# A four-network GNN kernel: the column loop of its PNA layers as straight code, with one wide maximum

## The reference, cut to what matters

```python
msg = concatenate([h[src], h[dst]], axis=-1) @ Mw.T + Mb
deg = segment_sum(ones(E), dst)
s1, s2 = segment_sum(msg, dst), segment_sum(msg * msg, dst)
mx, mn = segment_max(msg, dst), segment_min(msg, dst)
mean = s1 / deg
var = relu(s2 / deg - mean * mean)
std = sqrt(var + 1e-30)
agg = concatenate([mx, mn, std, var], axis=-1)
h_neigh = concatenate([agg, agg * (log(deg + 1) / 4), agg * (4 / log(deg + 1))], axis=-1)
u = concatenate([h, h_neigh], axis=-1) @ Uw.T + Ub
```

## Time and profile before

| | |
|---|---|
| median of 3 runs | 3951.08 us (3942.02 to 3959.58) |
| the profiled execution's own time | 3915.32 us |
| its span | 3913.5 us |
| PE busy | 2472.3 us (63%) |
| DVE busy | 2233.6 us (57%) |
| ACT busy | 692.3 us (18%) |
| POOL busy | 1258.7 us (32%) |
| mean granted TensorE clock | 0.785 |

### The profile page before, as it was taken

One profiled execution on the slowest core, in us unless ns is written; L12 is line 12 of the kernel. 1 busy time (PEld: TensorE's weight loads), 2 busy tenths in 40 slices (PEclk: granted clock), 3 DMA queues, 4 the chain that ended last, 5 costly groups with the idle time before them and its releaser, 6 DMA issues. The chain is left out here.

```text
span 3913.5 us, 50857 instructions
## 1 busy us (share of the span) xinstructions
PE 2472.3 (63%) x11996; PEld 1384.5 (35%) x11997; DVE 2233.6 (57%) x6995; ACT 692.3 (18%) x1557; POOL 1258.7 (32%) x1321
## 2 busy tenths in 40 slices
PE   6988879886968955455456654454448644544563
PEld 2444345743635532222224422222225322222242
DVE  6877766463353265555555645555556645555555
ACT  0235532411121030000001500000003300000112
POOL 3000000002000036666642155655640356555520
PEclk8999989997979977677678676766767867767785
DMA  3122366253523535444441144444430444444411
GB/s 109 50 93 109 142 210 230 99 206 124 176 81 138 176 100 179 159 163 159 138 145 40 53 160 144 160 155 135 157 113 1 141 136 160 154 134 158 153 43 45
DMA packets 152225, 511.54 MB, mean 131 GB/s; under 512 B 32194, under 2 KB 51552, under 8 KB 151248
## 3 DMA queue, kind: packets, MB, share of 16 engines
q1 hardware_dynamic: 94782, 350.03, 25.5%
q0 software_dynamic: 43536, 93.43, 8.6%
q10 hardware_dynamic: 13826, 67.12, 4.2%
HBM read 280.33 MB, written 230.13 MB: 130 GB/s over the span
## 5 line engine op out<-in xcount | busy, mean ns | idle before, releaser
L615 POOL DMA_INDIRECT rows_g<-a_dram,idx_now x1173 | 1133.3, 966 | 1566.8 <-DMA a_dram<-g 801.4
L1485 PE MATMUL psum<-hs,slab 128*128 128x384 bf16 x6600 | 1196.2, 341 | 166.2 <-issue 124.0
L1485 PEld LDWEIGHTS psum<-hs,slab 128*128 128x128 bf16 x6600 | 674.5, 102 | 711.2 <-issue 326.3
L1045 DVE SCALAR_TENSOR_TENSOR run<-run,mask_pt,rows_g 128x128 f32<-128x128 f32 x1170 | 405.6, 347 | 278.5 <-issue 224.7
L1048 DVE SCALAR_TENSOR_TENSOR run<-run,mask_pt,rows_g 128x128 f32<-128x128 f32 x1170 | 403.3, 345 | 34.6 <-issue 26.8
L1637 PE MATMUL psum<-identity,std_now 128*128 128x128 f32 x75 | 33.6, 448 | 598.1 <-ACT std_now L1341 512.9
L1432 PE MATMUL psum<-onehot_key,onehot_lane 128*128 128x512 bf16 (+1 forms) x1968 | 366.4, 343 | 60.9 <-issue 36.3
L726 DVE TENSOR_SCALAR onehot_key<-key_row,key_at 128x1600 bf16<-128x1600 f16 x492 | 310.2, 630 | 0.0
L1644 PE MATMUL psum<-w_U,vturned 128*128 128x384 f32 x150 | 119.2, 896 | 292.6 <-ACT vturned L1349 265.2
L1341 ACT ACTIVATE std_now<-var_now,eps 128x128 f32<-128x128 f32 x75 | 30.1, 401 | 1444.5 <-DVE var_now L1007 928.9
L1432 PEld LDWEIGHTS psum<-onehot_key,onehot_lane 128*128 128x128 bf16 x1968 | 160.4, 100 | 249.5 <-issue 55.0
(11 more groups left out here) (298 smaller groups left out, 3018.2 us busy)
## 6 DMA issues: line engine op xcount, KB each, us to landing
slab<-at_part SPq DMA_DIRECT2D x200, 800.0 KB
scan_dram<-run SPq DMA_DIRECT2D x291, 512.0 KB
at_part<-part_now ACTq DMA_DIRECT2D x50, 800.0 KB, 3.6
sums_dram<-run ACTq DMA_DIRECT2D x43, 576.0 KB, 2.9
rows_g<-a_dram,idx_now POOLq DMA_INDIRECT x1173
rows_g<-in_attr SPq DMA_DIRECT2D x43, 148.5 KB
a_dram<-g SPq DMA_DIRECT2D x3, 1600.0 KB, 7.7
agg<-sel_dram SPq DMA_DIRECT2D x3, 1600.0 KB
```

The costliest lines, as they stand in the source:

```text
L615: nc.gpsimd.indirect_dma_start(rows_g[:, slot, j, :], None, a_dram, bass.IndirectOffsetOnAxis(ap=idx_now[:, slot, j:j + 1], axis=0)).then_ ...
L1045: V.scalar_tensor_tensor(at[:, 0:D], before[:, 0:D], mark, rows, ALU.add, ALU.max).then_inc(s_run, 1)
L1485: T_.matmul(ps[:, 0:3 * D], counts[:, k * P:(k + 1) * P], hs[:, k, at:at + 3, :].rearrange("p s f -> p (s f)"), start=(k == 0), stop=False ...
```

## The change

The loops of POOL, DVE and ACT over the columns are written out, with constants in place of registers. A gather takes its index straight from `src_pt`; it may start once DVE has done the group four before. It writes the first half of a row in `rows_g`, which is now twice as wide; ACT writes the negated values into the second half (one operation for a group), and DVE makes one maximum of 256 values a column over both: the minimum is kept as the maximum of the negated values and turned back in the merges. The writes of `run` go out from ACT's queue, one group later, and SP only loads slabs.

Of a block, the own node's row is added to the sums by two identity products on PE; DVE has one reduction (`sums_of`), ACT the square of the mean, DVE one subtraction (`variance`), ACT Relu and root. Each step has a fixed group: the sums after group min(4b+3, 3b+24), variance and square one later, Relu and root two later, and both ACT's `var_turned(b)` and DVE's `take_part(b)` three later (two for the last two blocks). `take_part` has three operations; the biases' rows are added by a product with one row of ones into `bu`, for which PE's wait for the layer's weights moves ahead. Small tiles move into the unused third slab.

```diff
+def sums_at(b):
+    return min(4 * b + 3, 3 * b + 24)
+def take_at(b):
+    return sums_at(b) + (3 if b < NB - 2 else 2)
...
-        idx_now = sb("idx_now", [P, RING, Q], I32)
-        rows_g = sb("rows_g", [P, RING, Q, D], F32)
+        rows_g = sb("rows_g", [P, RING, Q, 2 * D], F32)
...
 @block.sync
-                with sp.Fori(0, TURNS) as turn:
-                    for k in range(2 * RING):
-                        write_runs(2 * RING * turn + RING, k)
-                        if k % RING == 0:
-                            half = k // RING
-                            load(2 * turn + (3 + half), 1 - half, turn + (1 + half))
+                with sp.Fori(1, NB // 2) as turn:
+                    for half in range(2):
+                        load(2 * turn + half, half, turn)
+                load(NB - 1, 0, NB // 2)
+                sp.wait_ge(s_run, T * l + T)
...
 @block.gpsimd
-                    pool.wait_ge(s_idx, GT * l + first + (k + 1))
+                for k in range(GT):
+                    slot = k % RING
+                    if k >= RING:
+                        pool.wait_ge(s_run, T * l + Q * (k - RING) + Q)
+                    elif l:
+                        pool.wait_ge(s_run, T * l)
+                        pool.wait_ge(s_st[slot], written_before(l, slot))
+                    for j, t in enumerate(cols_of(k)):
                         nc.gpsimd.indirect_dma_start(
-                            rows_g[:, slot, j, :], None, a_dram,
-                            bass.IndirectOffsetOnAxis(ap=idx_now[:, slot, j:j + 1], axis=0)).then_inc(s_gat[slot], 16)
+                            rows_g[:, slot, j, 0:D], None, a_dram,
+                            bass.IndirectOffsetOnAxis(ap=src_pt[:, t:t + 1], axis=0)).then_inc(s_gat[slot], 16)
...
 @block.vector
+                def sums_of(b):
+                    ps = psum[:, 1024 + 1024 * (b % 2):2048 + 1024 * (b % 2)].rearrange("p (k c) -> p k c", k=2)
                     dve.wait_ge(s_spmm, n + (NB * 5 + 4))
+                    V.tensor_reduce(var_tmp[:, 2 * (b % 2):2 * (b % 2) + 2, :],
+                                    ps[:, :, 0:3 * D].rearrange("p k (s f) -> p k f s", s=3), AX.X,
+                                    ALU.add).then_inc(s_agg, 1)
+                def variance(b):
+                    dve.wait_ge(s_mean_sq, n + 1)
+                    V.scalar_tensor_tensor(var_raw[:], var_tmp[:, 2 * (b % 2) + 1, :], rdeg[:, b:b + 1], mean_sq[:],
+                                           ALU.mult, ALU.subtract).then_inc(s_var, 1)
                 def take_part(b):
                     dve.wait_ge(s_vmm, n + 2)
-                    V.tensor_tensor(row(edge_sum, b), row(edge_sum, b), lrows[:, 0, :], ALU.add)
...
-                    V.tensor_tensor(u0, u0, lrows[:, 1, :], ALU.add).then_inc(s_vu, 1)
+                def columns(k):
+                    dve.wait_ge(s_minus_rows, GT * l + k + 1)
+                    if l or k >= RING:
+                        dve.wait_ge(s_st[slot], 16 * (k // RING) + written_before(l, slot))
+                    for j, t in enumerate(cols_of(k)):
+                        dve.wait_ge(s_run, T * l + t)
+                        V.scalar_tensor_tensor(at, before, mask_pt[:, t:t + 1], rows, ALU.add,
                                                ALU.max).then_inc(s_run, 1)
+                for k in range(GT):
+                    columns(k)
+                    for b in range(NB):
+                        if sums_at(b) == k:
+                            sums_of(b)
+                        if sums_at(b) + 1 == k:
+                            variance(b)
+                        if take_at(b) == k:
+                            take_part(b)
...
 @block.scalar
-                with act.Fori(0, NB) as b:
-                    deviations(b)
-                    var_turned(b)
+                for k in range(GT):
+                    slot, n = k % RING, len(cols_of(k))
+                    act.wait_ge(s_gat[slot], gathered_before(l, slot) + 16 * Q * (k // RING) + 16 * n)
+                    A.mul(rows_g[:, slot, 0:n, D:2 * D], rows_g[:, slot, 0:n, 0:D], -1.0).then_inc(s_minus_rows, 1)
+                    if k:
+                        write_runs(k - 1)
+                    for b in range(NB):
+                        if sums_at(b) + 1 == k:
+                            mean_squared(b)
+                        if sums_at(b) + 2 == k:
+                            deviations(b)
+                        if take_at(b) == k:
+                            var_turned(b)
+                write_runs(GT - 1)
...
 @block.tensor
+                if c >= CALLS:
+                    for ps, at in zip(banks, ats):
+                        T_.matmul(ps[:, 0:3 * D], identity16[:],
+                                  hs[:, ds(b, 1), at:at + 3, :].rearrange("p b s f -> p (b s f)"), start=False,
+                                  stop=False, skip_group_check=True)
...
                     T_.matmul(bank(6 + b % 2)[:, 0:2 * D], ft2[:, b * P:(b + 1) * P], weights["M"][:, D:3 * D],
-                             start=True, stop=True).then_inc(s_bu, 1)
+                             start=True, stop=False)
+                    T_.matmul(bank(6 + b % 2)[:, 0:2 * D], ones[0:1, :], both, start=False, stop=True).then_inc(s_bu, 1)
```

More of the change, by code:

```diff
@@ L272, in gnn_kernel @@
         esum = run[:].rearrange("p r q f -> p (r q f)")[:, 0:3 * EC * D].rearrange("p (s j f) -> p s j f", s=3, j=EC)
-        same = var_tmp[:].rearrange("p k f -> p (k f)")[:, 0:T]
-        same_turn = std_now
-        ecarry_t = vturned[:, 0:P + 1]
-        ecarry = var_now
+        beside = rows_flat[:, 4 * ET * P:]
+        same = beside[:, 0:T]
+        same_turn = beside[:, 512:512 + P]
+        ecarry_t = beside[:, 768:768 + P + 1]
+        ecarry = beside[:, 1024:1024 + P]
         s_last = sem("s_last")
@@ L964, in told @@
                     return V_LAYER * l + V_X3 + k
-                def take_indices(first, k):
-                    n = len(cols_of(k)) if isinstance(first, int) and first == 0 else Q
-                    V.tensor_copy(idx_now[:, k % RING, 0:n], src_pt[:, ds(Q * first + Q * k, n)]).then_inc(s_idx, 1)
-                if l:
-                    dve.wait_ge(s_run, 2 * T * l)
-                for k in range(RING):
-                    take_indices(0, k)
                 for b in range(NB):
@@ L1023, in take_part @@
-                    dve.wait_ge(s_take, 3 * n + 6)
-                    V.tensor_tensor(u0, u0, lrows[:, 1, :], ALU.add).then_inc(s_vu, 1)
-                def columns(turn, k):
-                    slot = k % RING
-                    whole = turn is None
-                    i = k if whole else 2 * RING * turn + (RING + k)
-                    n = len(cols_of(k)) if whole else Q
-                    rounds = k // RING if whole else 2 * turn + (1 + k // RING)
-                    full = 16 * Q * rounds
-                    dve.wait_ge(s_gat[slot], full + (gathered_before(l, slot) + 16 * n))
-                    dve.wait_ge(s_st[slot], 16 * rounds + written_before(l, slot))
-                    for j in range(n):
+                    dve.wait_ge(s_take, 2 * n + 2)
@@ L1046, in columns @@
                                                ALU.max).then_inc(s_run, 1)
-                        dve.wait_ge(s_run, steps)
-                        V.scalar_tensor_tensor(at[:, D:2 * D], before[:, D:2 * D], mark, rows,
-                                               ALU.subtract, ALU.min).then_inc(s_run, 1)
-                    if not whole or k + RING < GT:
-                        dve.wait_ge(s_run, 2 * Q * i + (2 * T * l + 2 * n))
-                        if whole:
-                            take_indices(0, k + RING)
-                        else:
-                            take_indices(2 * RING * turn + RING, k + RING)
@@ L1057, in _ @@
-                for k in range(RING):
-                    columns(None, k)
-                variances(0, 0)
-                with dve.Fori(0, TURNS) as turn:
-                    for half in range(2):
-                        for k in range(RING * half, RING * half + RING):
-                            columns(turn, k)
-                        take_part(2 * turn + half)
-                        variances(2 * turn + (half + 1), 1 - half)
-                for k in range(FIRST, GT):
-                    columns(None, k)
-                    if k in (FIRST + 1, FIRST + 4):
-                        b = 2 * TURNS + (k - FIRST) // 3
-                        take_part(b)
-                        variances(b + 1, (b + 1) % 2)
+                for k in range(GT):
[7 more added lines that the diff above has]
+                            take_part(b)
@@ L1072, in _ @@
                 take_part(NB - 1)
                 dve.wait_ge(s_last_turned, l + 1)
[L1075 to L1077 removed]
+                for e in range(2):
+                    last = V.tensor_tensor_scan(carry_t[:, e, 1:P + 1], mask_turn[:], bank(0)[:, e * P:(e + 1) * P],
```

(12 more changed lines are left out.)

131 lines of the change are left out of this document (46 added, 85 removed).

## The result

The changed kernel takes 4015.75 us (4009.18 to 4026.22, 4 runs) where the kernel before takes 3953.57 us (3942.02 to 3959.58, 4 runs): a ratio of 1.0163, 95% interval 1.0131 to 1.0196, so it is slower by 62 us. Its profiled execution took 4009.18 us for a span of 4007.2 us. The profiled execution of before was 38 us under its median and this one 7 us under, so the two profiles differ by more, 93.7 us, than the medians. Most of the experiments ran on chips where both kernels are far faster, because nothing is held up there beside the gathers; each of them stands beside the kernel before on its own chip.

The account below looks back on a forecast made before the run. Bound by a chain: POOL's gathers plus pauses for late index copies. Gathers 1485, pauses 442 and ends' wait 63 make 1990 against 1951.8 us, +38, so 3951 + 38 = 3989 us; range 3800 to 4235.

Parts of the forecast that it names:

- The hold-up: Gather streaks some 7 us old: PE's counts unseen until 2.8 us (up to 4.3) after the streak ends; DVE's sequencer crawls.
- The gathers' pace (3523): Rival, column loops: pauses were only the loops' own, so straight code runs at 1485 + 39 us; -428, chance 0.14.
- the rule of the Trainium skill, "Runtime: NRT & Kernel Launch", section "Instruction fetch mechanics": Taken branches out of a two-page window stall fetch; by that, straight code would remove all DVE's issue, giving 3523.
- The pause for each block, 6.4 us in 69: Column loops: POOL stops after 16 gathers for DVE's late take_part, 6.4 us a block, 442 us in all.
- their count is written at 8.4 us, beyond the age: PE's products in a block, counted 8.4 us (7.5 to 8.7) after POOL's restart, too late to be seen at once.
- seen in time in some blocks: Rival, column loops: some blocks' PE products are seen within the streak; -28, 3923 us, chance 0.20.
- The pause after a late transpose: Rival, column loops: transposes' count also late, ACT stands in var_turned; 9.8 us a block, +262, 4213 us, chance 0.14.
- The bias product: 256-column PE product, 25 a layer beside the first streak: under 1.0 us each, 0 in the sum.
- The ends' wait: POOL's wait for the last run writes before the ends' gathers: raised from 53.0 to 63 us.
- The wide maximum: One 256-wide DVE maximum a column: 467 ns, 0.50 us with release against 0.53 for two; saves nearly nothing.
- The 1485 us of the gathers: POOL in the three loops: 1173 gathers at 1.27 us from start to start, unchanged by the change.
- pauses and start: Column loops: 69 pauses of 6.4 us (442) replace 414 us of pauses; the start stays the same.

Follow-up runs that it names:

- y2: The kernel before, unchanged, profiled again on a chip where nothing is held up: 3383.73 us, one run.
- x1: Changed kernel without the product that adds the bias rows (part of the answer left out), nothing held up: 3386.35 us, ratio 1.0006 to before.
- w3: The kernel before with only the bias rows' product added in place of DVE's two operations, counts held up: 3924.03 us, ratio 1.0057 to before.
- y1: The changed kernel, unchanged, on a chip where nothing is held up: 3456.62 us, ratio 1.0206 to before.
- y3: Changed kernel with bias rows added by two DVE operations again, without the one-row product, nothing held up: 3393.13 us, ratio 1.0026 to before.
- w1: z1 with the 256-wide maximum split into two of 128, on a chip where counts are held up: 3936.85 us, ratio 1.0087 to before.
- z1: Changed kernel with bias rows on DVE and run writes on SP's queue again, nothing held up: 3392.28 us, ratio 1.0030 to before.
- y4: Changed kernel with the run writes on SP's queue again, nothing held up: 3446.04 us, ratio 1.0187 to before.
- x4: Changed kernel with the blocks' DVE and ACT calls and PE's transposes and products with U out of the loop: 3447.46 us, one run.
- x3: Changed kernel with POOL filling 256 unused values after each group of four gathers, nothing held up: 3532.52 us, ratio 1.0426 to before.

## Why the prediction was nearly right, and where it was not

Forecast were 3989 us and 0.47 for slower; measured were 4015.75 and 62 us instead of 38. The time fell inside the range, but in good part by luck: the pattern of the pauses was another one, and what was missed lies in terms put at 0 and +10.

**The hold-up: there, but only half described, and its cause open.** In an older streak the others go on waiting for PE until some microseconds past its end. The prediction put this to counts that are not seen and left PE's matmuls at their usual pace. In the result that fits 18 of 36 waits; in the other 18 the transposes themselves end late, because PE itself crawls ahead of them, at up to 2.9 us a matmul. The kernel before had this in the stretch of the earlier trace rows too: 11 matmuls of the block products in the 2 us from 890.61, then one every 0.7 to 2.8 us until 915.09.

y2 tests what the hold-up costs, and whether it is the code's: the same instructions with the same gathers, and 531 us less, 1951.8 - 1531.7 = 420 of them in the loops. Of the other 111, 28 are lost ahead of the edge gathers, where DVE's busy time is about half of y2's only from 25 to 75 us, at the program's first 25 gathers and just behind them; 23 come between the start of the edge gathers and the first loop, and 61 behind the three loops, where 25 gathers each stand. So it is not the code alone, and the time is lost beside gathers and just behind them. The lower clock of the held-up kind is not what costs the time: PE's busy time in a loop is 322 to 324 us there and 314 to 315 in y2.

That the gathers cause it rests on these times; no run changed them where the hold-up is. A rival stays untested: that the sequencers of PE, DVE and ACT are all slowed together, instead of PE's counts being kept back. What makes an execution one or the other is open too; it went with the chip (3383 and 3384 on two, 3901 and 3954 on others), and x1's one long execution, without a profile, is the only one that left its chip's level. Everything in the prediction was argued for the kind that the result was measured on.

**The gathers' pace (3523), given 0.14.** Straight code alone did not bring it, and the rule of the Trainium skill, "Runtime: NRT & Kernel Launch", section "Instruction fetch mechanics", explains nothing where nothing is held up: the looped kernel runs at the gathers' pace in y2. Where PE crawls it does not fit either: in the result's profile the two instruction queues moved 103 packets in all, and PE has 296 issue gaps ahead of one line. Where nothing is held up both kernels are at that pace, and the change still loses 2%.

**The pause for each block, 6.4 us in 69: the pattern failed, the sum held.** The step "their count is written at 8.4 us, beyond the age" was sized too late: it is seen at 7.6 us, so every other block passes, and the second has its transposes late. This is the rival "seen in time in some blocks", in every second block. Two blocks take 40.9 + 11.7 = 52.6 us, against 2 x 26.7 = 53.4 by the forecast: less than 1 us a block between them, but not for the priced reason, so that the sum held is luck. The pause after a late transpose was put at 9.8 us and is 11.2 to 13.2: ACT goes on 4.3 to 6.5 us after a streak of 32, not 2.8; the other steps (0.4, 2.9, 1.0, 2.0) are as worked out. In POOL's idle time: 33 pauses of 11.8 are 390 us, where 442 were forecast; 67 us of waits after the first 16 gathers come to them.

**The bias product: mis-sized, the largest miss.** "Under 1.0 us, beside the first streak, 0 in the sum." At the full clock it adds little: the first blocks follow each other at 1.26 us instead of 0.8 on the mean. But with it PE has no gap left, the granted clock falls from 1.00 to 0.50, and the rest follow at 2.30 us: 32.7, 25.6 and 25.7 us more for the 25 blocks, where the prediction had at most 25. And the cover was never the 41 us of the first streak: in both kernels POOL needs DVE's first columns after 16 gathers, and the streak of before is 32 long only because DVE comes in time. With DVE late, POOL stands 27.5, 19.8 and 19.8 us. An estimate from these rows: 24 steps of 1.26 us would be 30.2 us instead of 52.5, 45.4 and 45.5, and the waits some 5 us each, so most of the late start is the clock. In place of DVE's two operations it costs 22.6 us where counts are held up (w3) and 63.5 us where not (y1 to y3).

**The ends' wait: +10 forecast, +34.6 measured.** The timelines of PE, DVE and POOL at the end of the last loop, whose last gather ends at 3789.26:

```profile
3797.44 8.66 PE L1469 MATMUL psum<-hs,slab 128*128 128x384 bf16 x48
...
3797.68 0.35 DVE L995 SCALAR_TENSOR_TENSOR ft<-psum,log,ft 128x128 f32<-128x128 f32 x1 [22.47 <-PE psum L1636]
...
3809.08 0.35 DVE L995 SCALAR_TENSOR_TENSOR ft<-psum,log,ft 128x128 f32<-128x128 f32 x1 [5.29 <-PE psum L1636]
...
3812.88 1.52 DVE L1016 SCALAR_TENSOR_TENSOR run<-run,mask_pt,rows_g 128x256 f32<-128x256 f32 x3
...
3818.91 0.95 POOL L625 DMA_INDIRECT hs<-scan_dram,end_idx  x1 [29.66 <-DMA scan_dram<-run]
```

From the last gather to DVE's take_part at 3797.68 it is 8.4 us (PE ends the transposes at 3794.20, 4.9 us after the last gather; then the copy and the products). Then DVE's take_part at 3809.08 waits 5.29 us for the next block's products, and PE has a whole block of matmuls (8.66 us) ahead of them; the last columns stand behind that operation, end at 3814.40, and their write lands 4.5 us later. I had counted one late block after the last gather, and there are two, one after the other. In w1, on another chip, with the same order on DVE and the writes on SP's queue, the three waits are 15.7, 30.2 and 15.3 us, 61.2 in all; what share the queue has in that stays open.

**The wide maximum: 467 ns forecast, 485 measured;** no gain from it, as said. The gathers grew by 17 ns, 20 us in all, where I had left them as they were. Where nothing is held up there are more long gathers with the wide operation (over 1.06 us, 251 of 1248 in y3, 90 in y2); in y3 they lie beside DVE operations for 0.68 of their time and the short ones for 0.50. DVE's company alone can lengthen a gather: the program's first 25 take mostly 1.11 us in y2, with DVE 22.3 of 25 us busy, and mostly 0.95 in the kernel before, with DVE at 10.1. The Trainium skill, "SBUF — State Buffer", section "SBUF: two separate sides", lets a two-input DVE operation and a GpSimd one that reads SBUF exclude each other, which would lengthen a gather that meets a longer operation. The runs don't settle it: with the wide operation the mean is 983 ns in the result, 984 in x1, y1 and z1 and 986 in y3, but 972 in y4, 979 in x4 and 969 in x3; with narrow ones 963 in w1, 966 and 969 in the kernel before and w3, 975 in y2. The cause of the 20 us stays open.

**The sum.** The 1485 us of the gathers are 1173 x 1.266; with the rounded 1.27 that is written there they would be 1490, on both sides of the difference. By terms, in the two profiles: gathers +20 (forecast 0), pauses and start +37 (+28), ends +35 (+10), 92 against 38. Against the medians the miss is 62 to 38, since the profiled execution of before was a quick one. The experiments give a rough split on another chip of that kind (before 3901): w1, which leaves out the bias product, the queue and the wide operation, +35; the bias product, put into the kernel before, +23. That they nearly add up to 62 proves nothing, since they start from different kernels.

No version was faster than the kernel before: y3 and z1 are 0.3% slower where nothing is held up, and w1 0.9% where it is. None of them ran on the other kind.

## What to carry to other kernels

Ask of a stretch that covers a step what makes it as long as it is: here the cover itself hung on the engine that the step made late. Ask of a small product added to PE whether PE still has gaps, and read the granted clock of that stretch afterwards: here the clock, and not the product's columns, made most of the price. If an engine's count comes many microseconds after its instruction ended, ask what else is running beside it and whether that engine itself still issues at its usual pace, and look at the same program on another chip before the code is blamed. And taking work from an engine that waits (DVE, 355 to 250 us busy) pays nothing: the pauses moved from one releaser to the next, at nearly the same total.

## What the runs showed of the hardware

Beside a streak of indirect gathers an execution can be of one of two kinds. In the one, a count of PE is seen 0.2 us after the product, 13 us into the streak (865.57 to 865.73). In the other it is seen up to 24.5 us later (890.77 to 915.24), PE issues a matmul only every 0.7 to 2.9 us in the older part of the streak (455.1 us of issue ahead of one line, 35.4 in the other kind), and DVE's own issue gaps are 224.7 us instead of 38.5. The kernel before takes 3383 to 3384 us in the one and 3901 to 3954 in the other.

An fp32 product of 256 columns with one row of weights costs as much as one with 128 rows: 0.63 us each at a granted clock of 1.00, 1.15 us each at 0.50, two passes counted together. With it ahead of each loop (the result, y1 and w3, three layers each) the clock fell from 1.00 to 0.50 all nine times while PE was busy without a gap; without it (the kernel before and y3, three layers each) it stayed at 1.00 all six times, and PE had gaps.
